# A two-layer decoder kernel: gate products ordered chunk by chunk over four batches, with two context weight blocks added first

## What is computed

```
q, k, v = x, ctx, ctx                    # k and v are the same tensor
xin = concatenate([q, k, v], axis=-1)    # 4 x 256 x 768
ig  = xin @ Wi + bi                      # 768 x 16 weights, one column a head
fg  = xin @ Wf + bf
log_f = log_sigmoid(fg);  F = cumsum(log_f);  D = exp(F_s - F_t + ig_t - max)   # per head, t <= s
h = ((q k^T / 4) * D / normalizer) @ v ; per-head norm
```

## Time and profile before

| | |
|---|---|
| median of 3 runs | 1132.42 us (1131.62 to 1134.52) |
| span of the profiled execution (the profile gives no other total of it) | 1133.0 us |
| PE busy | 1029.7 us (91%), 5986 matmul records |
| PE weight loads busy | 825.7 us (73%) |
| DVE busy | 732.4 us (65%) |
| ACT busy | 574.6 us (51%) |
| POOL busy | 466.2 us (41%) |
| DMA | 85.59 MB, mean 76 GB/s |
| the gates block, from PE's first gate record to the next block's first matmul | 745.9 to 781.8 us of the span |

### The profile page before, as it was taken

The page is one execution under the profiler, slowest core; times in us unless marked ns, Lnnn a source line. Parts: engine busy times, 40 slices in busy tenths (PEclk is TensorE's granted clock), DMA queues, the critical chain, the costliest instruction groups (busy, mean ns, idle before and its releaser), DMA issues. The chain is left out here.

```text
span 1133.0 us, 18735 instructions
## 1 busy us (share of the span) xinstructions
PE 1029.7 (91%) x5986; PEld 825.7 (73%) x5986; DVE 732.4 (65%) x2146; ACT 574.6 (51%) x1568; POOL 466.2 (41%) x481
## 2 busy tenths in 40 slices
PE   8999999998995699579899999988978889999995
PEld 5888888887873699547778888845444568877784
DVE  5988887883675366446656672126686657788875
ACT  3454555445221355346667772037875546655553
POOL 5777777861277344455111110010135313444322
PEclk9999999999997899879999999988998989999998
DMA  6631111000011799626101101001003011112101
GB/s 217 235 132 61 29 30 28 19 12 1 1 54 56 237 354 333 196 69 186 37 25 61 30 15 38 1 21 50 2 1 114 0 56 56 57 56 75 38 1 38
DMA packets 83495, 85.59 MB, mean 76 GB/s; under 512 B 8545, under 2 KB 75943, under 8 KB 83280
## 3 DMA queue, kind: packets, MB, share of 16 engines
q1 hardware_dynamic: 79056, 75.39, 20.4%
q0 software_dynamic: 3072, 7.34, 2.2%
q10 hardware_dynamic: 1280, 1.77, 0.5%
HBM read 63.36 MB, written 22.02 MB: 75 GB/s over the span
## 5 line engine op out<-in xcount | busy, mean ns | idle before, releaser
L547 POOL TENSOR_TENSOR a_qk<-h,a_by_sin 128x512 f32<-128x512 f32 x64 | 86.6, 1353 | 5.0
L334 DVE CUSTOM_DVE_ANT_0 h<-a_score_ps,mask_bf 128x128 f32<-128x128 f32 (+1 forms) x128 | 40.7, 355 | 62.0 <-PE a_score_ps L327 62.0
L306 ACT ACTIVATE a_probsT<-a_turn_ps 128x384 f32<-128x384 f32 x128 | 61.3, 479 | 36.1 <-PE a_turn_ps L265 36.1
L1265 POOL TENSOR_TENSOR a_w_l<-a_w,a_w_h 128x256 fp32r<-128x256 f32 x30 | 21.8, 727 | 113.1 <-ACT a_w_h L1458 112.9
L340 ACT ACTIVATE y_moe<-y_moe,a_nmax 128x128 f32<-128x128 f32 x64 | 25.7, 402 | 82.8 <-DVE a_nmax L334 82.5
L434 PEld LDWEIGHTS a_proj_ps<-a_w,xT 128*128 128x128 f32 x512 | 62.0, 192 | 3.2 <-issue 1.2
L434 PE MATMUL a_proj_ps<-a_w,xT 128*128 128x128 f32 x512 | 62.5, 275 | 0.4 <-DVE hT L492 0.4
L1004 POOL TENSOR_TENSOR e_w_l<-e_w,e_w_h 128x512 fp32r<-128x512 f32 x32 | 40.9, 1278 | 52.3 <-ACT e_w_h L1072 52.3
L76 PE MATMUL a_proj_ps<-a_x_l,a_w_h 128*128 128x512 f32 x128 | 55.8, 436 | 2.6 <-ACT a_v L572 0.8
L728 PE MATMUL t_y_ps<-wo,attnT 128*128 128x256 f32 x256 | 57.6, 381 | 0.0
L2513 POOL TENSOR_TENSOR m_up_l<-m_up_w,m_up_h 128x1024 fp32r<-128x1024 f32 x8 | 19.5, 2434 | 89.4 <-ACT m_up_h L2485 89.4
(11 more groups left out here) (439 smaller groups left out, 3373.6 us busy)
## 6 DMA issues: line engine op xcount, KB each, us to landing
slots<-zeros SPq DMA_DIRECT2D x4, 2048.0 KB, 7.1
e_rows<-slots SPq DMA_DIRECT2D x32, 256.0 KB, 4.7
e_w<-in_L_ffn_w_dram SPq DMA_DIRECT2D x32, 256.0 KB, 4.9
out_slots<-e_out SPq DMA_DIRECT2D x32, 256.0 KB, 4.3
e_w<-in_L_ffn_w_dram SPq DMA_DIRECT2D x32, 128.0 KB, 4.3
a_w<-in_L_attn_w_q_dram SPq DMA_DIRECT2D x32, 128.0 KB, 2.3
m_up_w<-in_up_dram SPq DMA_DIRECT2D x8, 512.0 KB, 3.8
a_w<-in_L_attn_Wq_dram SPq DMA_DIRECT2D x16, 128.0 KB, 2.3
```

The costliest lines, as they stand in the source:

```text
L306: act.activation(self.probsT[:, b % 2, :], self.turn_ps[:, b % 2, 0:CAUSAL], ACT.Copy).then_inc(self.turned_kept, 1)
L334: done = dve.tensor_tensor_reduce(self.probs[:, b, cells], self.score_ps[:, r, cells], self.k.mask_bf[:, cells], -1.0, 3e38, ALU.add, ALU. ...
L547: pool.tensor_tensor(qk[:, par, 0 if what == "q" else 1, half * HALF:(half + 1) * HALF], by_cos[:, r, :], by_sin[:, r2, :], ALU.add).then_ ...
```

## The change

In `layer1_gates`, PE's loops over batch and chunk are swapped: for each chunk, the four batches (strips) come one after another. The chunks are 4 (`2 * DC`) in place of 6: DVE first adds, in place, the weights of chunks 4 and 5 to those of chunks 2 and 3, for f and then for i, and PE waits for that sum ahead of chunk 2 of each gate. DVE's two additions stand ahead of its other work in the block, behind a wait for the loads of the weights.

```
+        w_joined = m.sem("g_w_joined")
...
             def _(pe):
                 pe.wait_ge(k.ctx1_in, k.ctx1_loads)
                 pe.wait_ge(k.xT_ready, k.xT_count)
-                for ps, w in ((f_ps, k.w_f), (i_ps, k.w_i)):
-                    for b in range(B):
-                        for c in range(GATE_K):
-                            moving = k.xT if c < DC else k.cT
+                for n, (ps, w) in enumerate(((f_ps, k.w_f), (i_ps, k.w_i))):
+                    for c in range(2 * DC):
+                        if c == DC:
+                            pe.wait_ge(w_joined, n + 1)
+                        moving = k.xT if c < DC else k.cT
+                        for b in range(B):
                             last = pe.matmul(ps[b * ROWS:(b + 1) * ROWS, 0:S], w[:, c, :],
-                                             moving[:, c % DC, b * S:(b + 1) * S], start=c == 0, stop=c == GATE_K - 1,
+                                             moving[:, c % DC, b * S:(b + 1) * S], start=c == 0, stop=c == 2 * DC - 1,
                                              tile_position=(0, b * ROWS))
                     last.then_inc(gates, 1)
...
             def _(dve):
...
+                dve.wait_ge(k.ctx1_in, k.ctx1_loads)
+                for w in (k.w_f, k.w_i):
+                    dve.tensor_tensor(w[:, DC:2 * DC, :], w[:, DC:2 * DC, :], w[:, 2 * DC:GATE_K, :], ALU.add
+                                      ).then_inc(w_joined, 1)
                 for c in range(DC):
                     dve.wait_ge(x_high, c + 1)
```

## The result

The changed kernel took 1119.53 us in the median of 4 runs (1115.56 to 1122.04), the kernel before 1132.79 us beside it (1131.62 to 1134.52). The ratio is 0.9872, with a 95% interval of 0.985 to 0.9894: 14.5 us (12.0 to 17.0) less; the two medians themselves are 13.3 us apart. Two later series, on two chips, gave 0.9855 (0.9827 to 0.9882) and 0.9885 (0.9862 to 0.9907).

A forecast was written before the change was run, and what follows sets the result against it. PE was taken to bound the block through gate products, 32 stacks and tail. 11.4 - 0.1 (waits) - 0.06 (DVE late) = 11.2 us took the median from 1132.4 to 1121.2 us, range 1119.3 to 1123.2.

The forecast's parts named there:

- the slot count: Gate matmul records on PE, counted in slots of 0.427 us (low clock) or 0.219 us: 68 become 16, 11.4 us earlier.
- Four strips at once: Gate products: 64 records run four side by side, as the mix's 24 records within 0.86 us suggest, making 16 slots.
- The two-strip rival: Gate products: only two strips run at once, 32 slots, gain 7.9 us, 1124.5 us; chance 0.09.
- What is late next: ACT, DVE and SP behind the gates: stacks remain the longest way; DVE 0.06 us late, taken up by four banks.
- The additions and waits: DVE's two additions, 214 ns each, cost nothing; PE's two new waits for the sum cost 0.1 us together.
- I take zero: Code behind the block moves as a whole; shifted low-clock stretches there count as zero, one worth up to 1.7 us either way.
- an earlier rise of the clock: Gate products: the clock rising two microseconds earlier would give about 1 us more.
- one late stretch: Behind the block: one low-clock stretch falling differently is worth up to 1.7 us, either way.
- the serial one: Gate products: no more records side by side than one, 64 slots, gain 0.9 us, 1131.5 us; chance 0.03.
- the one with the low clock until the stacks' end: Gates and stacks: clock stays low, 64 stack records at 0.427 us, 2.2 us slower, 1134.6 us; chance 0.02.

The follow-up runs named there:

- Both parts alone: Against the kernel before: loops swapped, six chunks, no sum, 1118.92 us; context weights summed first, batch after batch as before, 1126.61 us.
- both orders at the full clock: Kernel before and changed kernel, each with unused bf16 matmuls added in three places to keep PE busy: 1131.32 us and 1121.17 us.
- the padded one: Changed kernel with 13 more matmuls on one strip ahead of each gate, results unused: 1134.51 us, ratio 0.9989 to the kernel before.
- filler: Unused bf16 matmuls added to the changed kernel at the gates block's end, 1115.92 us; with two also behind each transpose pair in the block before, 1115.83 us.
- the other places: Changed kernel with unused bf16 matmuls at the recurrence's end alone, 1121.15 us; there, between the earlier block's transposes and at the gates block's end, 1121.17 us.

## Why the prediction was right and where it was wrong

- **PE's gate products bound the block, and the slot count priced them.** Right: 68 slots to 16, 11.39 us forecast for the first stack, 17.33 - 5.83 = 11.50 us measured. Both parts alone, and both orders at the full clock, follow the same count.
- **Four strips at once, read from the mix.** Right: loads come in fours at one distance of 0.43 us. The two-strip rival would have needed 32 slots and a gain of 7.9 us. The Trainium skill's rule on row groups ("TensorE: Matmul & The Clock Gate", Part 3) doesn't hold for these strips. Its 3.07x, given there for four row strips, is not the factor of these four column strips either: 64 records fit 16 slots, a factor of about 4.
- **What is late next.** Right to 0.2 us, counted from the first gate record: ACT read `f_ps` at +3.70 (forecast 749.58 - 745.92 = 3.66), first stack at +5.83 (5.94), g at +8.01 (7.98), the recurrence's first matmul at +24.45 (24.7).
- **The additions and waits.** 0.23 and 0.22 us against 0.214, hidden; the waits cost nothing against 0.1 us.
- **Behind the block: "I take zero".** This step failed. The forecast let everything behind the block move as a whole, and put the low stretches there at zero, with 1.7 us either way for one of them. The runs show 3.2 to 3.7 us less in every profile of the changed kernel (347.5 to 348.0 us in place of 351.2), less low-clock time over its 16 runs, and both back again with the padded one. 11.5 + 3.4 = 14.9 us, against 14.5 us measured. What places the low stretches stays open, as said above, and no row of before told the sign. But the size could be read: the clock behind the block stood at 0.89 and 0.85 over 133 us, in more stretches than the one that was priced. The range's lower end, 1119.3, didn't even hold the prediction's own two terms, about 1 us for an earlier rise of the clock and 1.7 us for one late stretch, which make 1118.5.
- **The rivals.** The two-strip one, the serial one and the one with the low clock until the stacks' end didn't happen; the clock rose in the middle of the gates for i, as it had for f before. The low-clock one had priced a stack record at 0.427 us, which is the distance of gate records; no run shows stacks at the low clock.

## What to carry to other kernels

Where small f32 matmuls go to different strips of columns, put the strip innermost: the gain is the ratio of slots, and a seam between two strips in the trace of before already shows that they run side by side. When a stage in front gets shorter, don't move the rest as a block: list the low-clock time behind it and give the forecast's range its whole price, here 0.28 us per us. Where filler is tried, the places to begin with are those where PE would wait anyway and nothing waits for it: there it raised the clock here, though a shorter time was not shown; the other places gained little or nothing.

## What the hardware showed that I had not expected

The kernels' times scatter by 10 us within one chip (before: 1126.81 to 1136.91 us) with equal work, and low-clock time explains it down to 1.3 us over all 133 runs. The time behind the block lies at 351.1 to 351.4 or at 347.4 to 348.0 us in eight profiles of six kernels, with nothing between. These are single executions; over all runs a kernel with one code spreads wider than the 3.5 us between the groups.
